# The SSM's first batch is prepared inside the first FFN, and TensorE's convolution tile gets a PSUM bank of its own

## The reference

```python
x = x + attention(layernorm(x))        # one head, scores over 512 tokens
x = x + ffn(layernorm(x))              # 16 experts, top 4, all experts computed
x = x + mamba2(layernorm(x))           # the "SSM"
x = x + ffn(layernorm(x))              # the same weights again
# ffn, for every expert e:  h = t @ w1[e].T + b1[e];  s = swiglu(h)
#                           acc += route[e] * (s @ w2[e].T + b2[e])
# mamba2: zxbcdt = u @ W_in.T          -> z (256), xBC (512), dt (4 heads)
#         dt = softplus(dt + dt_bias);  xBC = silu(4-tap causal conv of xBC)
#         a scan over the tokens (state 128 x 64 for each head), y * silu(z), rms norm, W_out
```

## Time and profile before

| | |
|---|---|
| median of 3 runs | 748.96 us (747.16 to 749.07) |
| the profiled execution's own time | 746.62 us |
| its span, first to last instruction | 744.9 us |
| first FFN, batch 1 to tail | first matmul at 124.3, last at about 320.2 us of the span |
| SSM, first transposes to the last output matmul | 320.2 to about 555 us |

### The profile page before, as it was taken

How to read it: one execution, slowest core, us unless ns; L and a number is a source line. 1 busy time by engine, 2 the same in 40 slices (tenths; PEclk the granted TensorE clock), 3 DMA queues, 4 the chain that set the end, 5 groups by cost and what they waited for, 6 DMA issues and landing times. The chain is left out here.

```text
span 744.9 us, 13019 instructions
## 1 busy us (share of the span) xinstructions
PE 712.4 (96%) x3800; PEld 577.7 (78%) x3800; DVE 627.3 (84%) x1498; ACT 577.0 (77%) x1096; POOL 239.7 (32%) x389
## 2 busy tenths in 40 slices
PE   4999999999999999978999999999989999999997
PEld 3678788788788878757888888888768887887885
DVE  3568887999899899856779999899869999988986
ACT  2667677988988888847787787787668889888884
POOL 2336455000015010005677677677650000500000
PEclk9999999999999999999999999999999999999999
DMA  9000011645465555200000000000036455655661
GB/s 270 2 2 4 4 37 60 227 181 175 170 200 179 176 171 204 86 0 1 2 1 2 4 3 2 9 3 2 31 140 207 176 202 186 206 184 173 222 202 39
DMA packets 29237, 77.19 MB, mean 104 GB/s; under 512 B 4884, under 2 KB 9455, under 8 KB 29167
## 3 DMA queue, kind: packets, MB, share of 16 engines
q1 hardware_dynamic: 29012, 76.36, 30.6%
q10 hardware_dynamic: 154, 0.00, 0.0%
HBM read 73.73 MB, written 2.62 MB: 102 GB/s over the span
## 5 line engine op out<-in xcount | busy, mean ns | idle before, releaser
L684 ACT ACTIVATE s_ring<-ps,b1T 128x512 f32<-128x512 f32 x256 | 172.6, 690 | 37.8 <-PE ps L1591 36.6
L1110 DVE SCALAR_TENSOR_TENSOR s_ring<-s_ring,top_col,r_all 128x1024 f32<-128x1024 f32 x128 | 165.3, 1292 | 23.7 <-ACT s_ring L684 22.6
L1117 DVE TENSOR_TENSOR s_lo<-s_ring,s_hi 128x1024 fp32r<-128x1024 f32 x128 | 156.2, 1220 | 3.0 <-ACT s_hi L690 3.0
L690 ACT ACTIVATE s_hi<-s_ring 128x1024 fp32r<-128x1024 f32 x128 | 135.1, 1056 | 8.0 <-DVE s_ring L1110 7.5
L1565 PE MATMUL ps<-s_hi,w_hi 128*128 128x512 f32 x256 | 102.0, 399 | 2.8 <-DVE s_lo L1117 2.8
L1589 PE MATMUL ps<-ffn_hi,w_hi 128*128 128x512 f32 x256 | 103.9, 406 | 0.0
L1567 PE MATMUL ps<-s_hi,w_lo 128*128 128x512 f32 x256 | 101.3, 396 | 0.0
L1566 PE MATMUL ps<-s_lo,w_hi 128*128 128x512 f32 x256 | 101.2, 395 | 0.0
L1591 PE MATMUL ps<-ffn_hi,w_lo 128*128 128x512 f32 x256 | 101.1, 395 | 0.0
L1590 PE MATMUL ps<-ffn_lo,w_hi 128*128 128x512 f32 x256 | 101.1, 395 | 0.0
L1565 PEld LDWEIGHTS ps<-s_hi,w_hi 128*128 128x128 f32 x256 | 48.1, 188 | 17.4 <-DVE s_lo L1117 6.1
(11 more groups left out here) (232 smaller groups left out, 1552.2 us busy)
## 6 DMA issues: line engine op xcount, KB each, us to landing
r_all<-route_dram SPq DMA_DIRECT2D x128, 512.0 KB, 4.0
out_dram<-X SPq DMA_DIRECT2D x8, 256.0 KB, 4.4
X<-in_L_attn_a_x_dram SPq DMA_DIRECT2D x1, 1536.0 KB, 10.1
rows_f<-route_dram SPq DMA_DIRECT2D x48, 32.0 KB, 2.9
w_rows<-in_L_ffn_mlp_w_dram SPq DMA_DIRECT2D x1, 1024.0 KB, 6.4
route_dram<-route_cols SPq DMA_DIRECT2D x64, 8.0 KB, 1.5
X<-in_L_attn_a_x_dram SPq DMA_DIRECT2D x2, 256.0 KB, 3.0
in_rows<-in_L_attn_b_W_in_dram SPq DMA_DIRECT2D x1, 384.0 KB
```

The costliest lines, as they stand in the source:

```text
L684: eng.activation(s_ring[q % NR][:, e % 2, :], bank(e % 4), ACT.Silu, bias=b1T[:, e:e + 1], scale=ALPHA).then_inc(F["act"], 1)
L690: eng.activation(s_hi[q % NR][:, :, :], s_ring[q % NR][:, :, :], ACT.Copy).then_inc(F["hi"], 1)
L1110: eng.scalar_tensor_tensor(out=s_ring[q % NR][:, :, :], in0=s_ring[q % NR][:, :, :], scalar=top_col[:, 0:1], in1=r_all[q % NR][:, :, :], o ...
L1117: eng.tensor_tensor(s_lo[q % NR][:, :, :], s_ring[q % NR][:, :, :], s_hi[q % NR][:, :, :].bitcast(F32), ALU.subtract).then_inc(F["lo"], 1)
```

## The change

- TensorE, VectorE, ScalarE and GpSimd do the front half of the SSM's batch 0 behind pairs of the first FFN: statistics (2,5), `ssm_xn` (3,3), `u_turn` (3,7), `u_out` (4,0), `u_low` (4,1), the four `z_proj` at (4,3), (4,6), (5,1), (5,4), each `z_out` a pair later, `dt_arg` (6,0), `dt_exp` (6,2), `softplus` in halves at (6,5) and (7,1), `z_silu` (6,6), `project_in` (7,4) and (7,5), `conv_first` (7,7). Each figure is (batch, pair).
- They use banks 4 and 5. `conv(0, 0)` writes bank 7 and stands in the tail behind pairs 0 and 1; `conv(0, 1)` follows the tail. Neither waits for `conv_tap`.
- The six `conv_tap` stand behind VectorE's tail. `seg_sum(0, 0)` and `(0, 1)` stand ahead of `conv(0, 1)` rather than in step 0. `turn_sum` of batch 7 goes to bank 3 and `y_skip(0, 0)` waits for its `add_sum`.
- uT of batch 0 lies in `ffn_hi`/`ffn_lo` of batches 0 and 1, zs of batch 0 in the rows of the SSM's weights. `neg_A` is negated ahead of the FFN.

```diff
@@ late_router of VectorE
+                elif F is F1 and (b, q) == (2, 5):
+                    ssm_stats(0)
+                elif F is F1 and (b, q) == (3, 3):
+                    ssm_xn(0)
+                elif F is F1 and (b, q) == (4, 1):
+                    u_low(0)
+                elif F is F1 and (b, q) == (6, 0):
+                    dt_arg(0, 0)
+                elif F is F1 and (b, q) == (6, 5):
+                    softplus(0, 0, 0)
+                elif F is F1 and (b, q) == (7, 1):
+                    softplus(0, 0, 1)
@@ ffn_all of VectorE
-                    if F is F1 and b == 6:
-                        ssm_stats(0, early=True)
                     ffn(F, b, b == 0, after_pair=lambda q: late_router(R, F, b, q))
+                ffn(F, NB, False, True)
                 if F is F1:
-                    ssm_xn(0, early=True)
-                ffn(F, NB, False, True)
+                    for k in range(2):
+                        for shift in range(1, CONV_W):
+                            conv_tap(0, k, shift)
@@ late_router of ScalarE
+                if F is F1 and (b, q) == (NB - 1, 7):
+                    conv_first(0, 0)
+                    conv_first(0, 1)
+                if F is F1 and (b, q) == (NB, 2):
+                    conv_out(0)
+                elif F is F1 and (b, q) == (4, 0):
+                    u_out(0)
+                elif F is F1 and (b, q) in ((4, 4), (4, 7), (5, 2), (5, 5)):
+                    z_out(0, 0, ((4, 4), (4, 7), (5, 2), (5, 5)).index((b, q)))
+                elif F is F1 and (b, q) == (6, 2):
+                    dt_exp(0)
+                elif F is F1 and (b, q) == (6, 6):
+                    z_silu(0, 0)
@@ late_router of TensorE
+                elif F is F1 and (b, q) == (3, 7):
+                    u_turn(0)
+                elif F is F1 and (b, q) in ((4, 3), (4, 6), (5, 1), (5, 4)):
+                    z_proj(0, ((4, 3), (4, 6), (5, 1), (5, 4)).index((b, q)))
+                elif F is F1 and b == NB - 1 and q in (4, 5):
+                    project_in(0, q - 4)
+                elif F is F1 and b == NB and q < 2:
+                    conv(0, 0, q)
@@ conv of TensorE
+                    if b:
+                        wait(eng, M["conv"], 6 * b + 3 * k + 3)
+                    elif k == 0:
+                        eng.wait_ge(F1["x"], NB - 1)
+                    else:
+                        eng.wait_ge(F1["acc_sb"], NB)
@@ step of TensorE
+                if i == -1:
+                    seg_sum(0, 0)
+                    seg_sum(0, 1)
                 if first:
                     conv(i + 1, 1, 0)
```

More of the change, by code:

```diff
@@ new lines, in conv_out, with xs_silu @@
+            def conv_out(b):
+                j = PE_TILES[0]
+                wait(eng, M["cv_ps"], NJ * b + 3)
+                wait(eng, M["xs"], 3 * b)
+                eng.activation(conv_acc[:, j, :], bank(7), ACT.Identity, bias=conv_bias[:, j:j + 1]).then_inc(M["raw"], 1)
+            def xs_silu(b, par):
+                wait(eng, M["conv"], 6 * b + 6)
+                wait(eng, M["raw"], b + 1)
+                wait(eng, M["y_ps"], NT * (b - 1))
+                for first, count in ((PE_TILES[0], 1), (DVE_TILES[0], len(DVE_TILES))):
+                    eng.activation(xs[:, par, first:first + count, :], conv_acc[:, first:first + count, :],
+                                   ACT.Silu).then_inc(M["xs"], 1)
@@ L817, in conv_out @@
[L817 to L829, removed]
@@ L1238, in ssm_xn @@
-            def ssm_xn(b, early=False):
-                if isinstance(b, int) and b == 0 and not early:
-                    return
-                wait(eng, M["rstd"], 2 * b + 2)
-                wait(eng, M["uT_ps"], b)
-                for r in range(NT):
-                    eng.tensor_scalar(xn[:, r, :], X[:, b, r, :], ln1_mv[:, r, 0:1], ln1_rs[:, r:r + 1],
-                                      ALU.subtract, ALU.mult).then_inc(M["xn"], 1)
-            ffn_all(R1, F1)
-            eng.wait_ge(prep3_sb, PREP3)
@@ L1371, in step @@
                     cb_out(i, 0)
-                if first:
+                if first and i >= 0:
                     ssm_xn(i + 1)
@@ L1606, in ffn, with product, parts_of, u_of @@
                         after_pair(q)
+            def product(out, w, a, first=True, last=True):
+                eng.matmul(out, w[0], a[0], start=first, stop=False)
+                eng.matmul(out, w[0], a[1], start=False, stop=False)
+                return eng.matmul(out, w[1], a[0], start=False, stop=last)
+            def parts_of(t, *at):
+                return t[(slice(None), 0, *at)], t[(slice(None), 1, *at)]
+            def u_of(b, at):
+                return [part[:, at] for part in u_parts(b)]
@@ new lines, in u_turn, with project_in @@
+            def u_turn(b):
+                wait(eng, M["xn"], NT * b + NT)
+                wait(eng, M["raw"], b)
+                if b == 0:
+                    eng.wait_ge(S1["x1"], NB)
+                for r in range(NT):
+                    mm = eng.transpose(bank(7 if b else 4)[:, r:SEQ:NT], xn[:, r, :], ident[:, :])
+                mm.then_inc(M["uT_ps"], 1)
+            def project_in(b, k):
+                wait(eng, M["u_lo"], b + 1)
+                wait(eng, M["z_raw"], NT * b + NT - (k if b else 0))
+                if b == 0:
+                    eng.wait_ge(R1["route"], NB)
+                product(bank(7 - k if b else 5 - k), parts_of(bcT, k, slice(None)), u_of(b, slice(PAD, None))).then_inc(M["cv_ps"], 1)
@@ L1841, in step @@
                     cb_of(i, odd, 0)
+                if second and i > 0:
                     seg_sum(i, 0)
```

355 lines of the change are left out of this document (186 added, 169 removed).

## The result

The changed kernel takes **740.61 us** (median of 4 runs, 740.05 to 741.24), the kernel before 748.06 us (4 runs, 746.44 to 749.07). The ratio is 0.991, with a 95% interval of 0.989 to 0.9929. The forecast was 743.6 us. The profiled executions compare directly: 746.62 us before, 740.05 after (span 738.3), 6.57 us less. The gain is where it was looked for, but its terms differ from the forecast ones. One caution for all comparisons of profiled executions: the first FFN's first bias matmul starts anywhere from 134.77 to 137.03 us of the span in the 14 executions profiled here, although no experiment edits what stands ahead of it. Times of two executions are therefore compared as distances from a mark in each.

A forecast was written before the change was run, and what follows sets the result against it. TensorE, busy for 96% of the span, was taken as the bound. Terms: 10.2 - 3.9 + 0.3 - 1.2 = 5.4 us less, from the median 748.96 to 743.6 us; range 740.6 to 746.6.

The forecast's parts named there:

- a clock that stays up: Rival at the border: no half clock behind the long wait, same sum without 1.2 us, 742.4 us; chance 0.23.
- both waits gone: First FFN: waits at batch 6's bias matmul and for s_lo in batch 5 both vanish; bound of -1.1 us.
- border: From the end of the FFN's full pace to batch 1's transposes: 16.1 us against 26.3, 10.2 us less.
- matmuls in the FFN: First FFN: u_turn 0.6, four z_proj 1.9 and project_in 1.4 count in full on TensorE, 3.9 us more.
- waits in the FFN: Bias matmul of batch 6 waits about 0.8 instead of 0.36, batch 5's 0.74 for s_lo goes: 0.3 us less.
- clock behind the long wait: Behind a wait of about 3.4 us ahead of batch 1's transposes the half clock returns, costing 1.2 us.
- that leads to the second mark as before: Border chain from turn_sum through add_sum and ssm_xn(1) to batch 1's transposes, the second mark: 0.68 plus 4.69 us, unchanged.
- rival of the taps: Border: GpSimd's ramps and VectorE's taps hold each other up, up to 2.6 us given back, 746.2 us; chance 0.07.
- The 0.6 for `u_turn`: First FFN: four transposes added to TensorE, priced at 0.6 us by a row of the profile.
- the 0.47 for a `z_proj`: First FFN: three matmuls added to TensorE, priced at 0.47 us from the timeline, four times 1.9 us.
- VectorE's part at nothing: First FFN: added VectorE work, 5.4 us without cover, costs nothing because free time, added matmuls and rings hide it.
- The forecast of +5.5 us for the last `ffn_out`: End of the first FFN: its last ffn_out comes later than before by about 3.6 + 2.8 - 0.9 = 5.5 us.

The follow-up runs named there:

- Experiment 3: Changed kernel with GpSimd's step 0 held until VectorE's ssm_xn(1) is done; 739.82 us, ratio 0.9896.
- Experiment 7: Changed kernel with 15 more VectorE instructions of 0.2 us, results unused, behind pair 1 of batch 7; 746.15 us, ratio 0.9982.
- experiment 1: Kernel before with three small tiles (dt_tmp, dt_a, table_col) ahead of the FFN's, rings shifted 712 bytes, no instruction moved; 745.16 us, ratio 0.9975.
- experiment 5: Changed kernel with dt_exp, z_silu, the whole softplus and seg_sum back at the border; 738.35 us, ratio 0.9877.
- experiment 9: Changed kernel with batch 1's layer norm ahead of batch 7's addition, dt_exp at (6,3) and the second softplus half at (7,3); 735.11 us, ratio 0.9837.
- experiment 8: Kernel before with y_off hoisted, shifting the FFN's rings by 1,024 bytes, no instruction moved; 746.91 us, ratio 0.999.
- experiment 11: Changed kernel with the rings 1,024 bytes rather than 712 behind their place in the kernel before, no instruction moved; 741.98 us, ratio 0.9927.
- experiment 12: Kernel before with only table_col moved ahead of the FFN's tiles, a shift of 8 bytes, no instruction moved; 746.19 us, ratio 0.9983.
- experiment 4: Changed kernel with ssm_stats(1) and ssm_xn(1) ahead of batch 7's add_sum in VectorE's list; 736.76 us, ratio 0.9855.

## Why the prediction was nearly right

740.61 us stands at the very end of the stated range, 740.6 to 746.6, and that it holds is luck. That end was made of a clock that stays up, both waits gone and 1 us of scatter. The clock fell and one wait stayed; what brought the time there are terms that the prediction did not have, and the run that it started from. Its steps, against the profiled executions, each term by the trace:

| term | forecast | measured |
|---|---|---|
| border | 10.2 less | 26.28 - 17.61 = 8.7 less |
| matmuls in the FFN | 3.9 more | 3.2 more |
| waits in the FFN | 0.3 less | 1.00 - 0.36 - 0.74 = 0.1 less |
| clock behind the long wait | 1.2 more | 1.25 more |
| sum | 5.4 less | 4.35 less |
| places of the tiles, both FFNs | not foreseen | 0.55 + 0.67 = 1.2 less |
| waits in the SSM's later steps | not foreseen | 0.8 less |
| start of the first FFN | none | 0.2 less (135.54 to 135.31) |
| all | 5.4 less | 6.6 less |

**The border.** The mechanism was right up to `turn_sum`, 10.49 us for 10.7. The step that was mis-sized is "that leads to the second mark as before": 4.69 us from `add_sum` to the transposes became 335.87 - 329.43 = 6.44. The 4.69 were measured where GpSimd was idle; with the step sizes ready early, its product and ramps come at the very moment of `ssm_xn(1)`. Experiment 3 shows that cause for the product and the ramps together, by taking them away. The rival of the taps had the pair of engines right, GpSimd's ramps against VectorE, and the place wrong.

**The FFN's charge.** Two prices were too high. The 0.6 for `u_turn` is the length of a row, before whose end the next matmul starts; the 0.47 for a `z_proj` was taken right behind a wait. In the stream `u_turn` costs 219.00 - 218.65 = 0.35 us, and a `z_proj` 230.84 - 230.48 = 0.36. With four of these and 1.4 for `project_in` that is 3.2. How the FFN's part splits into matmuls, waits and places is known to some 0.2 us only: the matmul behind a wait or behind transposes is itself 0.1 slower, which the table leaves out.

**VectorE's part at nothing** held: no wait for s_lo over 0.1 us in the first FFN. Experiment 7 shows how near it was. The two waits came as forecast, 1.00 us at the bias matmul for 0.8, and none over 0.1 in batch 5.

**The clock** was right in this execution, and the mean granted clock of all four runs of the change is 0.995. But experiments 1, 5 and 9 show that it is partly chance, so that the 1.2 us is no sure price.

**Not foreseen.** The places of the tiles: the mark at 318.26 is 182.95 us behind the first bias matmul (before 315.95 - 135.54 = 180.41), so 2.54 more, where 3.2 - 0.1 = 3.1 were due; and the second FFN with its tail is 0.67 shorter. Experiments 1, 8, 11 and 12 show it; experiment 1 alone has 0.65 for each FFN. In the SSM, from `decay_sums(1)` to the second FFN, 192.99 us for 193.80: a wait of 0.4 us for uT is gone and one of 1.1 for y is 0.6. Both waits are unchanged in experiments 1, 8 and 12 and shorter in every version with the change's order, experiment 11 too, so the order did it and not the places; which part of it stays open. The 0.2 at the start of the first FFN is scatter of where an execution starts. The forecast of +5.5 us for the last `ffn_out` came to 323.62 - 319.98 = 3.6: 1.3 of the difference for these reasons, and the rest because the waits that left the tail were worth more than the 0.9 put down for them. The tail took 319.98 - 315.95 = 4.03 us before and 323.62 - 318.26 = 5.36 after, 1.33 more where 1.9 was forecast.

**The starting point.** The forecast is 3.0 us too high. 1.2 of it is the difference of the sums, 6.6 and 5.4. The other 1.8 is in what the forecast started from: the median of the three runs shown, 748.96, is 2.3 above the execution of 746.62 that the terms come from, and the median of the change only 0.6 above its own profiled one. The mean granted clock sorts these times. Beside the experiments the kernel before ran 72 times: 28 runs with a mean clock of 0.992 or 0.993 took 747.94 to 749.28 us, and 44 with 0.996 to 0.998 took 745.90 to 747.55. The profiled execution had 0.996. The clock of the run of 748.96 is not on record, but its time is one of the first group. Over the 17 to 27 runs beside experiments 1 to 8 the median was 747.36 and 747.10.

## What to carry to other kernels

Ask of each duration in a chain what the other engines did when it was measured, and whether the change puts something beside it: the four instructions that had been 1.11 us were 2.99 once GpSimd's work came early. When a train of waits is removed, look for work queued behind the wait that is left but ready long before it: moving one layer norm up was worth 3.8 us, half as much as the whole change, and only behind it did the step sizes in the FFN pay. A change that hoists a buffer shifts its neighbours; run the shift alone before the gain is put down to the order. And look at the granted clock of each run before medians are compared: a median of three or four runs can be that of one clock level by chance.

## What the runs showed of the hardware

- **VectorE beside GpSimd.** Each of the four `tensor_scalar` of 128x128 took 0.34 us with GpSimd idle; beside a product and two ramps they took 0.33 to 1.08 us (median 0.91), and 1.11 us for all four again when GpSimd waited. The Trainium skill ("SBUF — State Buffer", Who interferes with whom) says that the two engines share a pair of ports that one instruction locks for its whole length, and names `tensor_scalar` among those that can take it. By that rule `ssm_xn(1)` stands while GpSimd's instructions have the ports, and the trace agrees: 1.9 us are lost beside 0.62 + 2.04 us of GpSimd's work. Weighed against the place where the 4.69 us were measured, it would have pointed to this term.
- **The clock is no fixed function of the wait.** The same order gave 31.14, 29.49, 32.35 and 31.08 us from `turn_sum(6)` to `turn_sum(7)` (kernel before, experiments 1, 8 and 12). Behind a wait of 2.62 us for the taps the clock fell in the first and the last and stayed up in the second. In experiment 8 it was at half already ahead of that wait, which was 2.03 us there, with no wait over 1.46 us before it:

```profile
325.00:328.00 3.00, 2.43 (x9) 1.87 (x8) 0.35 (x2) 0.78 (x2) 0.00 (x0) 0.50 0.00 0
```

  It fell behind 1.93 us in experiment 5 and behind 1.58 us in experiment 9, and stayed up behind 1.57 us in experiment 4. The groups of runs of one kernel, 2 us apart for the kernel before and 4 us in experiment 5, go with it: the mean granted clock of each run tells them apart.
- **8 bytes.** The place of the FFN's tiles, 8 bytes on, is worth 0.54 us in a second FFN of 165.25 us; 712 bytes 0.67, 1,024 nothing. In the changed kernel 1,024 bytes rather than 712 cost 0.54 (experiment 11). TensorE's waits in the second FFN are the same to 0.1 us with 8 bytes as without. At the same granted clock whole runs differ by 2.2 to 2.4 us with 8 bytes, twice what the two FFNs show. Which tile's place counts, and by what mechanism, stays open.
